# Perceiver layer on one core: the last 8 MB of context in column blocks, first residual and statistics by chunk, normalisation in halves, four banks for one set of transposes

## The reference

```python
x = x + _L0_xattn_ref(_layernorm(x, axis=-1), ctx_4096, ...)      # fake_quant(x1) @ fake_quant(x2)
x = x + _L0_attn_ref(_layernorm(x, axis=-1), L0_attn_Wq, L0_attn_Wkv, L0_attn_Wo)
x = x + _L0_ffn_ref(_layernorm(x, axis=-1), L0_ffn_qweight, L0_ffn_qzeros, L0_ffn_scales, L0_ffn_bias)

def fake_quant(x, scale, zp):
    s = scale.reshape(()); z = zp.reshape(())
    q = jnp.clip(jnp.round(x / s + z), QMIN, QMAX)
    return (q - z) * s
```

## Time and profile before

| | us |
|---|---|
| median of 3 runs | 435.19 (433.32 to 437.91) |
| the profiled execution, whole | 433.4 |
| its span, first to last instruction | 431.7 |
| mean granted PE clock (1 is full) | 0.974 |
| PE / DVE / ACT / POOL busy | 379.1 / 323.9 / 220.6 / 38.0 |
| DMA, bytes moved | 77.44 MB |

### The profile page before, as it was taken

How to read it: one execution, slowest core, us unless ns; L and a number is a source line. 1 busy time by engine, 2 the same in 40 slices (tenths; PEclk the granted TensorE clock), 3 DMA queues, 4 the chain that set the end, 5 groups by cost and what they waited for, 6 DMA issues and landing times.

```text
span 431.7 us, 4679 instructions
## 1 busy us (share of the span) xinstructions
PE 379.1 (88%) x1830; PEld 280.0 (65%) x1836; DVE 323.9 (75%) x316; ACT 220.6 (51%) x266; POOL 38.0 (9%) x75
## 2 busy tenths in 40 slices
PE   0296768776999999999999999999689999999996
PEld 0121322324888877877878868887468878888884
DVE  4699888769842794773955946896999899999922
ACT  2968988986144585474763925412725233444000
POOL 8995000000000000000000001000000000000000
PEclk9998898998999999999999999999699999999999
DMA  7999999994263443535255414999800000000022
GB/s 279 425 424 420 420 421 424 419 390 176 70 222 111 131 162 106 188 102 186 103 183 207 155 40 173 282 201 243 313 2 2 2 0 0 2 0 2 0 97 97
DMA packets 24274, 77.44 MB, mean 179 GB/s; under 512 B 1626, under 2 KB 1802, under 8 KB 19210
## 3 DMA queue, kind: packets, MB, share of 16 engines
q1 hardware_dynamic: 24092, 77.01, 50.0%
q10 hardware_dynamic: 160, 0.13, 0.1%
HBM read 74.91 MB, written 2.10 MB: 178 GB/s over the span
## 4 chain that ended last, share of the span: by engine, by line
PE 70%; DVE 10%; DMA 10%; ACT 7%; issue 3%; SPq 0%; DVEq 0%; ACTq 0%
PE bank L1131 20%; PE bank L1004 12%; PE bank L1006 12%; PE bank L1005 12%; DMA ctx_more<-in_ctx 5%; DMA raw<-in_L_attn_Wo 4%; ACT q L423 4%; PE bank L965 2%; PE bank L1066 2%; PE bank L1091 2%; PE bank L997 2%; DVE q L683 2%; DVE stats L601 2%; PE bank L1079 1%; PE bank L1034 1%
## 5 line engine op out<-in xcount | busy, mean ns | idle before, releaser
L445 ACT ACTIVATE w_hi<-raw 128x2048 fp32r<-128x2048 f32 x29 | 55.3, 1911 | 49.3 <-DMA raw<-in_L_attn_Wo 28.2
L631 DVE TENSOR_TENSOR w_lo<-raw,w_hi 128x2048 fp32r<-128x2048 f32 x29 | 66.2, 2286 | 13.4 <-ACT w_hi L445 13.4
L1004 PE MATMUL bank<-w_hi,xt_hi 128*128 128x512 f32 x128 | 52.0, 406 | 0.0
L965 PE MATMUL bank<-q,at 128*128 128x512 bf16 x122 | 37.4, 429 | 16.3 <-DVE q L683 15.5
L1006 PE MATMUL bank<-w_hi,xt_lo 128*128 128x512 f32 x128 | 50.0, 391 | 0.0
L1005 PE MATMUL bank<-w_lo,xt_hi 128*128 128x512 f32 x128 | 49.9, 390 | 0.0
L1004 PE MATMUL bank<-w_hi,hd_hi 128*128 128x512 f32 x104 | 42.2, 406 | 5.6 <-DVE w_lo L631 5.6
L683 DVE TENSOR_SCALAR q<-q 128x2048 bf16<-128x2048 uint8 x32 | 38.7, 1226 | 6.6 <-ACT q L423 4.6
L1005 PE MATMUL bank<-w_lo,hd_hi 128*128 128x512 f32 x104 | 41.4, 398 | 0.0
L1006 PE MATMUL bank<-w_hi,hd_lo 128*128 128x512 f32 x104 | 41.2, 397 | 0.0
L469 ACT ACTIVATE work<-work,neg_mx 128x128 f32<-128x128 f32 x64 | 24.7, 387 | 23.4 <-DVE neg_mx L798 23.4
(11 more groups left out here) (153 smaller groups left out, 675.7 us busy)
## 6 DMA issues: line engine op xcount, KB each, us to landing
raw<-in_ctx SPq DMA_DIRECT2D x16, 1024.0 KB, 18.1
ctx_more<-in_ctx SPq DMA_DIRECT2D x16, 1024.0 KB, 17.8
raw<-in_L_attn_Wq SPq DMA_DIRECT2D x16, 1024.0 KB, 5.0
raw<-in_L_attn_Wo SPq DMA_DIRECT2D x13, 1024.0 KB, 5.1
raw_fifth<-in_L_attn_Wo SPq DMA_DIRECT2D x3, 1024.0 KB, 7.3
resid<-in_x SPq DMA_DIRECT2D x2, 1024.0 KB, 11.9
scale<-in_L_ffn_scales SPq DMA_DIRECT2D x16, 128.0 KB, 14.0
packed<-in_L_ffn_qweight SPq DMA_DIRECT2D x2, 1024.0 KB, 19.9
```

Of the source, the lines that this page charges most:

```text
L445: nc.scalar.activation(hi_slots[s], raw_slots[s], ACT.Copy).then_inc(w_hi_set, 1)
L631: nc.vector.tensor_tensor(lo_slots[s], raw_slots[s], hi_slots[s].bitcast(F32), ALU.subtract).then_inc(w_lo_set, 1)
L965: mm(bank[:, 4 * b + n, :], at[:, k, b * P:(b + 1) * P], q16[:, i % 2, n * CH:(n + 1) * CH], start=start, stop=False)
L1004: mm(bank[:, out_bank, :], x_hi, hi[:, c], start=first, stop=False)
```

## The change

The first 24 context tiles are loaded as before. The last 8 MB, row blocks 8 to 15 of batch 1, come as eight blocks of four row blocks by 512 columns: two for each chunk n of 512 columns, so that chunk 0 is complete after two of them. A block's piece for each partition is four runs of 2 KB, 1 MB in all. The last block is loaded in two halves with a semaphore each, and is rounded and converted in halves. PE's `ctx_block` has four matmuls into the one bank of the chunk and four column sums. After each pair of blocks DVE copies 32 rows of column sums (`colsums_of(n)`), PE runs `zero_point_of(n)` on 32 rows, and for chunks 0 and 1 `first_residual` with its statistics stands between the conversions. The norm is written in halves of 1024 columns, each with its count of `norm_set`, and `transposes` waits for the first half ahead of transpose 0 and for the second ahead of transpose 8. For this the rows of Wq, Wkv and the transposed norm are grouped by `(q p t)`: granule kq holds rows 512 kq to 512 kq + 511. Wo's new grouping names the same addresses as before. Batch 1's transposes have banks 1, 2, 3 and 5. On ACT, `upper_w(3)` stands after `sqrt_of(3)` and the copy of Wkv after `upper(1, g)`.

```diff
-    wq_rows = wq.rearrange("(p t) n -> p t n", t=KT)
+    ctx_rows = ctx_in[B - 1].rearrange("(t p) n -> p t n", p=P)
+    wq_rows = wq.rearrange("(q p t) n -> q p t n", q=4, t=4)
...
-            return 1 + g % 3 if n == 1 else 4 * (n % B) + g
+            return (1, 2, 3, 5)[g] if n == 1 else 4 * (n % B) + g
...
+                if i < CTX_ROWS:
+                    sp.dma_start(ctx_slots[i % CTX_RING], ctx_tiles[i]).then_inc(ctx_loaded[i % CTX_RING], 16)
+                else:
+                    n, k0 = (i - CTX_ROWS) // 2, KT // 2 + 4 * (i % 2)
...
+                        sp.dma_start(slot, ctx_rows[:, k0:k0 + 4, c]).then_inc(ctx_loaded[i % CTX_RING], 16)
...
-            for w in range(4):
+            round_last()
+            for w in range(3):
                 upper_w(w)
             sqrt_of(3)
+            upper_w(3)
+            for g in range(4):
+                upper(1, g)
             act.wait_ge(wkv_loaded, 16)
...
+            def normalise_halves(b):
+                for h in range(2):
+                    c = slice(h * D // 2, (h + 1) * D // 2)
+                    nc.vector.tensor_scalar(work[:, b, c], resid[:, b, c], mv[:, b, 0:1], rstd[:, b:b + 1],
+                                            ALU.subtract, ALU.mult).then_inc(norm_set, 1)
...
+            def colsums_of(n):
+                r = slice(P // NCH * n, P // NCH * (n + 1))
+                dve.wait_ge(ctx_mm, CTX_ROWS + 2 * n + 2 + (n == NCH - 1))
...
+                nc.vector.tensor_copy(colsum_at[r], bank[r, COLSUM_BANK[1], :]).then_inc(colsum_out, 1)
...
+            for g in range(3):
                 remainder(0, g)
-                if g < 3:
-                    convert_ctx(KT + 8 + g)
-            for i in range(11, 14):
-                convert_ctx(KT + i)
+                convert_ctx(KT + 8 + g)
+            colsums_of(0)
+            remainder(0, 3)
+            convert_ctx(KT + 11)
+            first_residual(1, 0)
+            convert_ctx(KT + 12)
+            colsums_of(1)
+            convert_ctx(KT + 13)
+            first_residual(1, 1)
             convert_ctx(KT + 14)
-            convert_ctx(KT + 15)
-            colsums(1)
+            colsums_of(2)
+            convert_last()
+            colsums_of(3)
             remainder_w(0)
-            for n in range(NCH):
-                ins = first_residual(1, n)
-            moments(1, ins)
+            first_residual(1, 2)
+            moments(1, first_residual(1, 3))
             reciprocal_sd(3)
-            normalise(1).then_inc(norm_set, 1)
+            normalise_halves(1)
             remainder_w(1)
...
+            def ctx_block(i, first=0, last=4):
+                n, k0 = (i - CTX_ROWS) // 2, KT // 2 + 4 * (i % 2)
+                r = P // NCH * n
+                pe.wait_ge(ctx_c, i + 1 + (first > 0))
+                for t in range(first, last):
+                    mm(bank[:, 4 + n, :], at[:, k0 + t, P:2 * P], q16[:, i % 2, t * CH:(t + 1) * CH],
+                       start=False, stop=False)
+                for t in range(first, last):
+                    ins = mm(bank[r:r + P // NCH, COLSUM_BANK[1], :], ones16[:, 0:P // NCH],
+                             q16[:, i % 2, t * CH:(t + 1) * CH], start=False, stop=k0 + t == KT - 1)
+                ins.then_inc(ctx_mm, 1)
...
-                    if n < B and t == 12:
-                        pe.wait_ge(lo_out, 4 * n + 1)
+                    if n == 0 and t == 12:
+                        pe.wait_ge(lo_out, 1)
```

More of the change, by code:

```diff
@@ L39 @@
 CTX_TILES = B * KT
+CTX_ROWS = CTX_TILES - KT // 2
 GROUPS = D // GROUPSIZE
@@ L509, in _ @@
             round_ctx(KT + 12)
-            for i in range(KT + 13, CTX_TILES):
+            for i in range(KT + 13, CTX_TILES - 1):
                 round_ctx(i)
-            for w in range(4):
+            round_last()
+            for w in range(3):
                 upper_w(w)
             sqrt_of(3)
+            upper_w(3)
+            for g in range(4):
+                upper(1, g)
             act.wait_ge(wkv_loaded, 16)
@@ L974, in ctx_tile, with zero_point, zero_point_of @@
                 ins.then_inc(ctx_mm, 1)
-            def zero_point(b):
-                pe.wait_ge(colsum_out, b + 1)
+            def ctx_block(i, first=0, last=4):
[9 more added lines that the diff above has]
+                ins.then_inc(ctx_mm, 1)
+            def zero_point():
+                pe.wait_ge(colsum_out, 1)
                 for n in range(NCH):
-                    mm(bank[:, 4 * b + n, :], sel[:, n, :], colsum_at, start=False,
+                    mm(bank[:, n, :], sel[:, n, :], colsum_at, start=False,
                        stop=True).then_inc(ctx_done, 1)
+            def zero_point_of(n):
+                r = slice(P // NCH * n, P // NCH * (n + 1))
+                pe.wait_ge(colsum_out, n + 2)
+                mm(bank[:, 4 + n, :], sel[r, n, :], colsum_at[r], start=False,
+                   stop=True).then_inc(ctx_done, 1)
             def transposes(n):
                 b = n % B
-                pe.wait_ge(norm_set, n + 1)
                 for t in range(KT):
                     g = t // 4
+                    if t % 8 == 0:
+                        pe.wait_ge(norm_set, 2 * n + t // 8 + 1)
                     if n < B:
-                        rows = work[:, b, :].rearrange("m (p t) -> m t p", t=KT)[:, t, :]
+                        rows = work[:, b, :].rearrange("m (q p t) -> m q t p", q=4, t=4)[:, g, t % 4, :]
                     else:
@@ L1177, in _ @@
             pe.wait_ge(sel_set, 1)
-            zero_point(0)
+            zero_point()
             pe.wait_ge(at_set, 2 * B)
-            for k in range(KT):
-                if k == KT // 2:
-                    transposes(0)
+            for k in range(KT // 2):
                 ctx_tile(1, k)
-            zero_point(1)
+            transposes(0)
+            for i in range(CTX_ROWS, CTX_TILES - 1):
+                ctx_block(i)
+                if i in (CTX_ROWS + 2, CTX_ROWS + 4):
+                    zero_point_of((i - CTX_ROWS) // 2 - 1)
+            ctx_block(CTX_TILES - 1, 0, 2)
+            ctx_block(CTX_TILES - 1, 2, 4)
+            zero_point_of(2)
+            zero_point_of(3)
             q_granule(0, 0)
```

56 lines of the change are left out of this document (38 added, 18 removed).

## The result

The changed kernel takes 437.28 us (median of 20 runs, 434.57 to 440.11) where the kernel before takes 434.48 (20 runs, 429.95 to 438.25): a ratio of 1.0078, 95% interval 1.0054 to 1.0101, so about 3.4 us slower (2.3 to 4.4) where 1.5 faster was forecast. The profiled execution took 437.0, its span 435.0 (before 433.4 and 431.7).

What follows compares the result with a forecast made beforehand. PE's own work was 70% of the span, so reaching batch 1's first q granule earlier shifts everything. Norm -0.44, handover -1.0, feed-forward norms -0.05 make -1.5 us: profiled 433.4 to 431.9, median 433.7; range 430.5 to 437.0.

Steps and rivals of the forecast that it cites:

- A PE block of four matmuls and four sums takes 1.37: PE's time for one context block in batch 1, 1.37 us, read from 84.28 to 85.65 in the earlier trace.
- the prediction's own mechanism: On DVE, conversions queue behind residuals waiting for PE's zero point; with the two pairs, the last conversion starts 2.7 us later.
- the list: DVE's instructions laid out in time from conversion 83.01 to the norm at 104.37, with PE's blocks and zero points.
- The moved residuals: Two residual/statistics pairs, 2.78 us, leave the stretch behind the last conversion; the norm comes only 0.44 us earlier.
- Copies of 32 rows: DVE's column-sum copies become four; each was taken at 0.69 us, like 128 rows, started 0.61 apart.
- Norm in halves, four banks: From batch 1's norm to PE's granule: halves of 0.70 us, no wait at transpose 12; gain 1.0 with the full clock.
- The full clock: Batch 1's sixteen transposes take 2.08 us, not 3.52, as PE idles 1.7 us ahead of them, not 4.0.
- Loads in runs of 2 KB: Eight context blocks land 2.71 us apart instead of 2.49; the delays are hidden, cost 0.
- The slow rival: Block loads become the bound: the norm slips from 2.89 us a landing; at 3.4 the time is 437.8; chance 0.13.
- The row pitch that was weighed: If pitch between partitions, not run length, slowed Wq's loads, blocks 8 KB apart would land every 2.49 us; sum unchanged.
- Slower: Measurable slowdown beyond about 1% (4.4 us), tied to blocks landing more than 3.6 us apart; chance 0.07.
- the price of a block: Load landing time of one context block: 2.71 us, taken from Wq's granules, between 2.49 and 3.0.

Runs made afterwards that it cites:

- e1: Changed kernel with a block's four column sums in four groups of 32 output partitions, zero point incomplete: 435.79 us, 0.9986 of the kernel before.
- e2: Kernel before with the last eight tiles' four column sums each aimed at one group of 32 output partitions: 436.92 us, 1.0035 of the kernel before.
- e4: Changed kernel with the residuals of chunks 0 and 1 each one conversion later, sums unchanged: 436.17 us, 1.001 of the kernel before.
- f2: Changed kernel with sums in four groups (zero point incomplete) and residuals of chunks 0 and 1 one conversion later: 432.83 us, 0.9956 of the kernel before.
- f3: Changed kernel with sums in four groups, residuals one conversion later and the complete zero point, computing the reference: 434.13 us, 0.9976 of the kernel before.
- e3: Kernel before with only norms in halves, four banks, regrouped weight rows and ACT's new order, no blocks: 435.17 us, 0.999 of the kernel before.
- h1: Changed kernel with batch 0's context norm whole again, other norms in halves: 437.60 us, 1.0053 of the kernel before.
- h4: Kernel before with norms in halves, four banks and new weight order, but batch 0's norm whole: 434.32 us, 0.9989 of the kernel before.
- f4: Kernel before with its last eight tiles loaded as four 128x512 pieces in 2 KB runs, pitch 8 KB: 436.38 us, 1.0007 of the kernel before.
- f1: Changed kernel, unchanged, timed again on another chip: 436.49 us, 1.0053 of the kernel before.

## Why the prediction was wrong

**The step that failed** is "A PE block of four matmuls and four sums takes 1.37", a term of the sum that was mis-sized: it measured 2.00. The duration was taken from the earlier trace rows, from a tile, and there the four sums aim at four groups of 32 output partitions (`r` steps with the chunk inside the loop). In `ctx_block` a chunk is fixed, so is `r`, and the four aim at one group. Same shapes, same count, 1.04 instead of 0.40, and a block is 2.00. The diff showed it: in `ctx_block` the line with `r` stands ahead of the loop over the sums, in `ctx_tile` inside it. The Trainium skill's "TensorEngine Tiling (Array Packing)", section Key Properties, has a rule that bears on it: tiles of the array (four of them, for 128 rows by 32 columns) are each tied to their partitions and work independently, so that different ones can run in parallel. The trace agrees, 0.40 for four groups against 1.04 for one.

A step of 0.64 became 3.24 between the first remainder and the norm because the prediction's own mechanism, conversions queued behind a residual that waits for PE, puts each block's sums into the round. After minus the list, both counted from the first remainder:

```
                     list    after   more
copy of sums 0        5.21    5.86   0.65
residual 0            7.85    8.85   1.00
conversion 28         9.24   10.25   1.01
residual 1           13.01   14.61   1.60
conversion 30        14.40   16.01   1.61
copy of sums 3       18.46   21.46   3.00
norm                 25.44   28.68   3.24
```
Ahead of residual 0 PE has three blocks in a row, 1.94 apart where DVE converts one every 1.74, and ends them 1.0 later than listed. The round to conversion 30 adds one block's 0.6, and the last two blocks, which nothing overlaps, add two and 0.1. The last 0.24 stand behind the last copy of 32 rows: `remainder_w(0)` starts 0.73 behind it and not 0.61, residual 2 another 2.32 later and not 2.19 (below). e1, e2, e4 and f2 show the cause: the sums moved to four groups take away 0.7 to 0.9% of the time in after (0.9986 against 1.0053 and 1.0078) and 0.5% in e4 (f2), moved to one they cost before 0.35%, and e4's order takes 0.4 to 0.7%.

**The moved residuals.** The forecast was that they give back ahead of the norm nearly all that they save (0.44 left of 2.78). The direction was right: even with the sums at 0.40 and the better order, f3 is only 0.41 ahead of before. The list itself was not tested to its end: with the sums at 0.40 and its order there is only e1, which agrees to 0.04 up to residual 0 and then has the lower clock. f2 and f3 come out near the list's 25.44 (25.27 and 25.47, before 25.88), but with the order of e4, so that is no proof of the list. That the order could be had without the wait was not looked for.

**Copies of 32 rows** take 0.68 to 0.70, as many as 128 rows: as taken from the earlier trace rows.

**Norm in halves, four banks.** 1.54 for both halves (0.70 each were taken), the sixteen transposes 2.19 without a stop at the twelfth and at the full clock, the granule released by `remainder_w(1)`, 3.80 behind the norm against 3.63 forecast. The size was right, and e3 shows it apart: 0.88 in the trace, under what the times resolve. The full clock was luck. It was forecast from 1.7 us of idle PE ahead of the transposes; in after it was 0.42, since `q_granule(0, 0)` itself ran mostly at the lower clock (0.63 over 104.8 to 109.4) and took 4.6 us where it takes 3.0 at the full one (e1, h1). Where that granule ran at the full clock and PE stood 1.98 to 2.01 (e1, e4, h1, h4), sixteen transposes took 3.2 to 3.6, and norm to granule 3.79 to 4.20.

**Loads in runs of 2 KB.** 2.71 was taken. ACT's timeline of after, against the earlier trace rows:
```profile
73.02 2.10 ACT L438 ACTIVATE q<-raw,prm,inv 128x2048 uint8<-128x2048 f32 x1 [0.62 <-DMA raw<-in_ctx]
75.74 2.10 ACT L438 ACTIVATE q<-raw,prm,inv 128x2048 uint8<-128x2048 f32 x1 [0.62 <-DMA raw<-in_ctx]
...
94.68 1.91 ACT L473 ACTIVATE w_hi<-raw 128x2048 fp32r<-128x2048 f32 x1 [0.75 <-DMA raw<-in_L_attn_Wq]
```
2.72 apart, granule 0 at 94.68 (94.66 was forecast), and no wait of DVE's for either. The slow rival did not happen. The row pitch that was weighed is not what slows these loads: after's and f4's have a pitch of 8 KB and come at 2.72, where 8 KB runs come at 2.49.

**What stays open** is what the other 1.40 costs, by which after was late at the first remainder. Its place is in the profile: PE begins the matmuls of tile 21 at 73.48 before and after, and the first remainder stands 5.45 behind that before and 6.85 after. PE's timeline of before:
```profile
73.48 1.04 PE L965 MATMUL bank<-q,at 128*128 128x512 bf16 x4 [1.74 <-DVE q L683]
```
That distance is 5.45 to 5.74 in the six profiles with the norm of batch 0 whole, and 6.79 to 6.89 in the eight with it in halves, where the lower clock stands in it. What moves from one execution to the next is when tile 21 begins, 72.00 to 75.90 over all of them: early in f1 (72.42), so that it is late by only 0.33, and late in h1 (74.76), which is late by 1.32 with the norm whole. The prediction priced the halves of this norm at nothing and did not look at PE there. In the times the whole norm gives back 0.12% in the mean and not the 0.32% that 1.40 us would be; whether the rest is noise or is lost again elsewhere no run here tells. Of the 3.4 us of the measured ratio (2.3 to 4.4), 2.80 - 0.87 = 1.9 have their place in the profile and a cause that runs bear out, 1.4 have a place only.

The range ended at 437.0 and the time is 437.28. "Slower" was given 0.07 and left to the loads, since the price of a block was one row read in one way; a bound from the other side, four matmuls one behind the other as in L965 (1.04 for four), would have put about 3 us on it (the 3.00 of the table).

## What to carry to other kernels

A duration read from a trace belongs to the instruction's operands, output partitions included, and not only to its shape and count: when a loop is turned round, check which index picks the group of partitions, and give neighbouring small matmuls different ones. On an engine that runs in order, put a step that waits for another engine behind one more piece of work that this engine needs next; here a line moved by one place was worth about half a per cent. When work is taken off the end of a path and put into a round trip ahead of it, price every member of the round as often as the round runs.

## What was not expected of the hardware

**Lower clock behind short stops of PE.** Ahead of tile 21 PE waits for the conversion behind the norm of batch 0. PE's timeline of after, then of h1:
```profile
73.48 1.04 PE L1022 MATMUL bank<-q,at 128*128 128x512 bf16 x4 [1.92 <-DVE q L720]
74.87 1.89 PE L1022 MATMUL bank<-q,at 128*128 128x512 bf16 x4
```
```profile
74.76 1.04 PE L1022 MATMUL bank<-q,at 128*128 128x512 bf16 x4 [1.74 <-DVE q L720]
```
and the windows of 73.4 to 80 (length, busy us of PE, PEld, DVE, ACT, POOL, granted clock, DMA), after and then h1:
```profile
73.40:80.00 6.60, 6.52 (x33) 2.52 (x34) 2.39 (x3) 4.11 (x3) 0.00 (x0) 0.74 1.05 387
```
```profile
73.40:80.00 6.60, 5.14 (x33) 2.40 (x34) 3.66 (x4) 4.32 (x3) 0.00 (x0) 1.00 1.05 387
```
With the norm in halves the stop is 1.92 or 1.93 and the mean clock of the window 0.74 to 0.79, in all eight profiles that have it; with the norm whole it is 1.74 and the clock 1.00, in all six. Each of the two windows holds 33 matmuls, busy 6.52 us and 5.14. Yet h1 is no faster than f1; in h1's profile a lower clock stood earlier instead, 0.87 over 60 to 73.4, where after has 1.00. The length of the stop alone doesn't decide it either: the clock fell behind 1.40 in e1 (below), not behind 1.74 in h1, behind 2.01 ahead of the transposes in h4 (3.62 for sixteen), and not behind 3.40 at the same place in e3 (2.20).

The same shows in e1's window of 90 to 100.5, and f2's with the same sums:
```profile
90.00:100.50 10.50, 9.94 (x28) 2.26 (x28) 6.64 (x9) 7.84 (x6) 0.00 (x0) 0.51 1.05 387
```
```profile
90.00:100.50 10.50, 8.21 (x43) 2.36 (x42) 9.26 (x12) 10.21 (x8) 0.00 (x0) 1.00 1.05 387
```

**DVE's overlap at a change of partitions.** An instruction starts 1.13 behind a conversion's start and 0.61 behind a copy's, but around a copy of 32 rows that starts at another partition than 0 it is later on both sides. DVE's timeline of after:
```profile
90.58 1.21 DVE L720 TENSOR_SCALAR q<-q 128x2048 bf16<-128x2048 uint8 x1
91.82 0.68 DVE L741 COPY work<-bank 32x512 f32<-32x512 f32 x1
92.53 1.23 DVE L720 TENSOR_SCALAR q<-q 128x2048 bf16<-128x2048 uint8 x1
```
1.24 and 0.71. The copy of chunk 0, at partition 0, has 0.61 behind it (86.19 to 86.80), and f3's copies of 128 rows have 0.59 (90.85 to 91.44). The Trainium skill's "VectorE: DVE Perf Modes", section "Two Vector instructions with no wait between them", lets an instruction begin early only where the two agree in such things as the quadrant they start in. The trace agrees: both rows start 0.03 behind the end of the one ahead, where they would start some 0.1 us sooner.
